# Moving the softmax sums' high parts to ScalarE and one key's row to GpSimd, with the sums' products two steps later

## The chip, the cores and the metric

One core of one Trainium2 chip. The metric is the device time of one execution in microseconds (us). The kernel before took 1920.23 us, the median of 3 runs (1919.83 to 1922.81).

## What is computed

A decoder layer: cross-attention of 16 x 56 tokens of width 256 over 1500 context tokens (16 heads of 128), then a mixture of 32 experts of which each token uses 4. The change lies in the attention alone. Cut to what matters:

```python
q = rms_norm(x @ q_w + q_b, nq_s)                    # 16 batches, 56 queries, 16 heads
k_img = rms_norm(img_ctx @ ki_w + ki_b, nki_s)       # image: context tokens 0..256 (257)
k_txt = rms_norm(txt_ctx @ k_w + k_b, nkt_s)         # text: context tokens 257..1499 (1243)
scores = q . k / sqrt(128)
attn = softmax(scores, axis=keys)                    # over image keys and text keys apart
out = sdpa(q, k_txt, v_txt) + sdpa(q, k_img, v_img)
```

Each softmax needs, per query and head, the sum of its exponentials over all keys. These sums are what the change deals with.

## The kernel before, in words

All products have 32-bit results at high precision: an operand is split into a high part, rounded to the format that TensorE multiplies fast (fp32r), and a low part, the rest; three products (high x high, low x high, high x low) stand for one.

The attention (`attend`) runs over 16 batches, `B`. A batch's context is cut into 13 tiles of up to 128 tokens: tiles 0, 1 and 2 are image, with 128, 128 and 1 token (tile 2, `LONE`, is the single key), tiles 3 to 12 are text. The 16 x 56 = 896 columns of queries and heads are taken in two halves of 448. A pair of a tile and a half is a **unit**; a batch has 26 (`UNITS`), numbered tile x 2 + half, so units 4 and 5 are the single key's. Every engine runs the same 26 **steps** per batch, with an order written out by hand in its own `body`:

- TensorE, step u: the scores of unit u (6 matmuls of 448 columns; for the single key 2), at even steps a "gram" product for the next tile (5 matmuls, lines 1150 and 1152), from which the keys' mean square comes, and the average of unit u-2 (lines 1143 to 1145 too). An ordinary unit has 12 matmuls in all, 6 for its scores and 6 for its average. The single key has no average on TensorE. The last two averages of a batch are carried into steps 0 and 1 of the next.
- ScalarE, step u: two exponentials of unit u-1, one to p_high (line 1322), one back to PSUM (1324), or one to lone_probs for the single key; c_high of a tile two ahead at even steps (`prepare`, 1303); high parts of the queries (`split_u`), copies of the averages (`copy_o`), and the copy of a sum's row out of PSUM (`copy_sum`, 1342).
- VectorE, step u: for unit u-1 (`take`) p_low (1405), the addition of the unit's exponentials to a running sum p_sum, 128 partitions x 448 (`add`, 1458 or 1461), and the copy of a bias to PSUM for a unit three ahead (`seed`, 1416). TensorE's scores of a unit wait for its seed, its average for p_low. At even steps also the mean square of a tile (`norm`, 1430, shown as junk<-psum,c_twice). It stands behind `take`, except at steps one before a sum's product (2, 4, 8, 10) and at step 6, where it stands ahead of it (`norms_first`). For the single key `take` adds lone_probs x its context row to o_raw (1447), and `add` works on one partition (1461, 1x448).
- GpSimd: at even steps key_rms (1611) of the tile whose mean square has just come; at odd steps c_low (1617) and c_twice (1630) of a tile two ahead. c_twice is the input of the next mean square. In between, at fixed steps, the query work of 128x896: `split_u` (u_low, 1661) at steps 2, 4, 12, 14, `scale_u` (1636) at 8, 10, 24 and 0, `scale_o` (1679) for the text of the batch before at 16 and 18 and for the image at 20 and 22, and `split_lone` (1667) at 17 and 19.
- SP issues the DMAs: tile loads, query loads, and the way of the sums: `store_sums`, `load_sums`, `store_reciprocals`, `load_reciprocals`, `store_o`, each at a fixed tile of its loop (`set_end`).

**The sums.** When the last unit of a half has been added, VectorE casts p_sum to its high part (`split_sum`, 1469) and subtracts to the low part (through `sub`, 1405). TensorE multiplies both with ones (`sums`, lines 1214 and 1215), into the same PSUM bank, `GRAM`, as the gram product, so it waits until the mean square of that bank has been read (`norm_summed`). ScalarE copies one row of the result, and the next gram waits for that copy (`sums_left`, `sum_copied`). The row goes to memory and back, VectorE takes reciprocals, and GpSimd multiplies the averages with them (`scale_o`). The text's sums of a batch are finished in the next batch. The steps are constants in lines 881 to 884:

```python
TEXT_SUM_SPLIT, TEXT_SUMS, TEXT_RECIP = (1, 2), (3, 5), 10
IMAGE_SUM_SPLIT, IMAGE_SUMS, IMAGE_RECIP = (7, 8), (9, 11), 16
```

The order in which the engines work in their steps is that of the calls in `body`; an engine waits in its order, and all behind a waiting instruction on it waits too.

## Time and profile before

| | before |
|---|---|
| median of 3 runs | 1920.23 us |
| the profiled execution | 1918.63 us |
| its span in the trace | 1916.8 us |
| TensorE busy (matmuls) | 1751.0 us, 91% |
| VectorE busy | 1397.1 us, 73% |
| ScalarE busy | 983.2 us, 51% |
| GpSimd busy | 1149.5 us, 60% |
| granted TensorE clock, mean | 0.973 of full |

In the tables PE is TensorE, PEld its weight loads, DVE VectorE, ACT ScalarE, POOL GpSimd, SPq the issue of DMAs from SyncE. The attention's batches run from about 250 to 1445 us; before them stand the projections, behind them the output product and the experts. Matmuls are pipelined, so a matmul's time in the trace is longer than the distance to the next; idle time counts on TensorE. The batch that the rows show begins at about 699 us and the next at about 774 us.

### The profile page before, as it was taken

Reading aid. Unit: us, or ns where it says so; the run is one execution under the profiler, and the core shown is the slowest. Engines: PE = TensorE matmul, PEld = TensorE weight load, DVE = VectorE, ACT = ScalarE, POOL = GpSimd, SP = SyncE. Lnnn points to the kernel's source line nnn. Section 1 sums busy time; section 2 is a strip of 40 time slices with the busy share of each in tenths; the row PEclk is TensorE's granted clock in tenths of the full one; section 3 lists DMA queues with packets and bytes.
Section 4 is the critical chain, followed back from the end, with each engine's and each line's share of the span. In section 5 each row is a group of like instructions: output and inputs, shape, how many; then the busy total and the mean of one; then the engine's idle time right before and its main releaser. Section 6 shows DMA issues by size and latency. Waiting matters only on the chain. (4 is left out here: it accounts for less than half of the span.)

```text
span 1916.8 us, 30691 instructions
## 1 busy us (share of the span) xinstructions
PE 1751.0 (91%) x8731; PEld 1534.5 (80%) x8731; DVE 1397.1 (73%) x2577; ACT 983.2 (51%) x1657; POOL 1149.5 (60%) x989
## 2 busy tenths in 40 slices
PE   7899979999999999999999999999992998699998
PEld 6566669889888888888898898888892886688887
DVE  4344477887978878878878879788782564577776
ACT  3444445555655655555555556556552553244443
POOL 1000278888788788788788887887862331133332
PEclk9999999999999999999999999999996999799999
DMA  3365564465564665554564665556436782133332
GB/s 110 121 208 197 194 183 111 107 116 123 123 120 114 130 121 117 122 135 114 116 132 108 116 126 125 116 116 131 98 90 195 252 274 92 66 107 115 116 109 78
DMA packets 417364, 251.19 MB, mean 131 GB/s; under 512 B 350272, under 2 KB 368832, under 8 KB 415520
## 3 DMA queue, kind: packets, MB, share of 16 engines
q1 hardware_dynamic: 417312, 250.55, 51.2%
q8 instruction: 26, 0.43, 0.1%
q14 instruction: 26, 0.21, 0.0%
HBM read 187.71 MB, written 60.10 MB: 129 GB/s over the span
## 5 line engine op out<-in xcount | busy, mean ns | idle before, releaser
L1322 ACT ACTIVATE p_high<-psum,key_rms 128x448 fp32r<-128x448 f32 x384 | 244.7, 637 | 397.1 <-PE psum L1145 397.0
L1143 PE MATMUL psum<-p_high,c_high 128*128 128x448 f32 (+1 forms) x768 | 287.8, 375 | 48.0 <-DVE p_low L1405 48.0
L1405 DVE TENSOR_TENSOR p_low<-psum,p_high 128x448 fp32r<-128x448 f32 x384 | 236.4, 616 | 100.2 <-ACT psum L1324 99.1
L1143 PE MATMUL psum<-u_high,c_high 128*128 128x448 f32 x768 | 285.5, 372 | 21.0 <-DVE psum L1416 15.1
L1144 PE MATMUL psum<-u_low,c_high 128*128 128x448 f32 x768 | 282.5, 368 | 0.0
L1145 PE MATMUL psum<-u_high,c_low 128*128 128x448 f32 x768 | 281.5, 366 | 0.0
L1145 PE MATMUL psum<-p_high,c_low 128*128 128x448 f32 (+1 forms) x768 | 281.5, 366 | 0.0
L1144 PE MATMUL psum<-p_low,c_high 128*128 128x448 f32 (+1 forms) x768 | 281.0, 366 | 0.0
L1416 DVE COPY psum<-beta_wide 128x448 f32<-128x448 f32 x416 | 259.4, 627 | 20.2 <-DMA beta_wide<-absorbed_biases 4.4
L1617 POOL TENSOR_TENSOR c_low<-stage,c_high 128x512 fp32r<-128x512 f32 x208 | 273.6, 1316 | 0.0
L1324 ACT ACTIVATE psum<-psum,key_rms 128x448 f32<-128x448 f32 x384 | 232.3, 605 | 0.0
L1611 POOL TENSOR_TENSOR key_rms<-key_ms,minus_half 128x1 f32<-128x1 f32 x209 | 118.9, 569 | 185.6 <-DVE key_ms L1430 183.3
L1143 PEld LDWEIGHTS psum<-p_high,c_high 128*128 128x128 f32 (+1 forms) x768 | 144.0, 188 | 72.8 <-DVE p_low L1405 62.1
L1461 DVE TENSOR_TENSOR p_sum<-psum,p_sum 128x448 f32<-128x448 f32 (+1 forms) x320 | 196.4, 614 | 0.0
L1143 PEld LDWEIGHTS psum<-u_high,c_high 128*128 128x128 f32 x768 | 144.8, 189 | 46.0 <-DVE psum L1416 20.6
L1630 POOL TENSOR_TENSOR c_twice<-stage,c_low 128x256 f32<-128x256 f32 x208 | 169.0, 812 | 16.3 <-POOL c_low L1617 2.4
L2024 POOL TENSOR_TENSOR scaled_gate<-gated,p_wide 128x448 f32<-128x448 f32 x64 | 83.5, 1306 | 155.8 <-ACT gated L2125 151.9
L1145 PEld LDWEIGHTS psum<-u_high,c_low 128*128 128x128 f32 x768 | 144.9, 189 | 12.5
L1145 PEld LDWEIGHTS psum<-p_high,c_low 128*128 128x128 f32 (+1 forms) x768 | 144.1, 188 | 12.1
L1430 DVE CUSTOM_DVE_ANT_0 junk<-psum,c_twice 128x257 bf16<-128x257 f32 x208 | 88.6, 426 | 89.3 <-POOL c_twice L1630 87.7
L1144 PEld LDWEIGHTS psum<-u_low,c_high 128*128 128x128 f32 x768 | 144.9, 189 | 10.9
L1144 PEld LDWEIGHTS psum<-p_low,c_high 128*128 128x128 f32 (+1 forms) x768 | 144.3, 188 | 8.6
(241 smaller groups left out, 4018.3 us busy)
## 6 DMA issues: line engine op xcount, KB each, us to landing
stage<-in_ctx SPq DMA_DIRECT2D x210, 256.0 KB, 2.8
averages<-o_raw SPq DMA_DIRECT2D x64, 448.0 KB, 5.2
o_stage<-averages SPq DMA_DIRECT2D x32, 896.0 KB, 5.4
u_raw<-absorbed_queries SPq DMA_DIRECT2D x60, 448.0 KB, 5.5
absorbed_queries<-u_stage SPq DMA_DIRECT2D x14, 1792.0 KB, 6.8
beta_wide<-absorbed_biases SPq DMA_DIRECT2D x32, 448.0 KB, 5.3
recip_wide<-reciprocals SPq DMA_DIRECT2D x32, 448.0 KB, 4.1
p_wide<-probs_by_expert SPq DMA_DIRECT2D x32, 448.0 KB, 3.6
```

What stands on the lines that cost most here:

```text
L1143: nc.tensor.matmul(out, high, rhigh, start=start, stop=False, **kw)
L1144: nc.tensor.matmul(out, high, rlow, start=False, stop=False, **kw)
L1145: return nc.tensor.matmul(out, low, rhigh, start=False, stop=stop, **kw)
L1322: nc.scalar.activation(p_high[:, probs_slot(u), :], src, ACT.Exp, scale=key_rms[:, t:t + 1])
L1324: nc.scalar.activation(out, src, ACT.Exp, scale=key_rms[:, t:t + 1]).then_inc(exp_done, 1)
L1405: return nc.vector.tensor_tensor(out, a, b, ALU.subtract)
L1416: nc.vector.tensor_copy(psum[:, bank_of(u), 0:HALF], beta_wide[:, s, cols_of(half)])\
L1430: nc.vector.tensor_tensor_reduce(out=junk[:, :], in0=psum[:, GRAM, 0:DIM + 1], in1=c_twice[:, slot(t, TWICE_RING), :], scale=1.0 / INNER, ...
L1461: added = nc.vector.tensor_tensor(total, part, total, ALU.add)
L1611: nc.gpsimd.tensor_tensor(key_rms[:, t:t + 1], key_ms[:, t:t + 1], minus_half[:, 0:1], ALU.pow)\
L1617: nc.gpsimd.tensor_tensor(c_low[:, k, :], stage[:, st, :], c_high[:, k, :].bitcast(F32), ALU.subtract)\
L1630: nc.gpsimd.tensor_tensor(c_twice[:, slot(t, TWICE_RING), 0:DIM], stage[:, st, nat], c_low[:, k, nat].bitcast(F32), ALU.add).then_inc(stag ...
```

## The change

ScalarE makes the high parts of the four sums of a batch (`high_sum`, new), at steps 1 and 2 for the text and 7 and 8 for the image; VectorE's cast is gone, its subtraction moves one step later. GpSimd adds the single key's row to the image's sums (`add_lone`, new), at steps 5 and 6; VectorE's add for it is gone, and its seeds no longer count it. The sums' products, the copies of their rows, the reciprocals and the image's scaling come two steps later. With the steps of the products, the steps at which the mean square stands ahead of `take` change too: 4, 6, 10 and 12 instead of 2, 4, 6, 8 and 10. SP's order stays.

```diff
--- before.py
+++ after.py
@@ -48,6 +48,8 @@
 PREP = 2
 UNITS = 2 * TILES
 AVERAGES = UNITS - 2
+
+ADDS = AVERAGES
 TOK = 112
 
 WB = DIM + 2
@@ -96,6 +98,11 @@
 def averaged(u):
 
     return u + 1 - min(max(u + 1 - 2 * LONE, 0), 2)
+
+
+def added(u):
+
+    return averaged(u)
 
 
 def probs_slot(u):
@@ -879,9 +886,11 @@
         O = 0
         IMAGE, TEXT = 0, 1
         TEXT_SPLIT, IMAGE_SPLIT = (1, 3), (10, 12)
+        TEXT_SUM_HIGH, IMAGE_SUM_HIGH = (1, 2), (7, 8)
+        LONE_ADDED = (5, 6)
         LONE_TERMS, LONE_HIGH, LONE_LOW = (12, 14), (14, 16), (17, 19)
-        TEXT_SUM_SPLIT, TEXT_SUMS, TEXT_RECIP = (1, 2), (3, 5), 10
-        IMAGE_SUM_SPLIT, IMAGE_SUMS, IMAGE_RECIP = (7, 8), (9, 11), 16
+        TEXT_SUM_SPLIT, TEXT_SUMS, TEXT_RECIP = (2, 3), (5, 7), 12
+        IMAGE_SUM_SPLIT, IMAGE_SUMS, IMAGE_RECIP = (8, 9), (11, 13), 18
 
         inverse_dram = nc.dram_tensor("inverse_rms", [B * TILES, 2, P], F32, kind="Internal").ap()
         negative_dram = nc.dram_tensor("negative_maxima", [B, 2 * HS // P, P], F32, kind="Internal").ap()
@@ -910,7 +919,7 @@
         u_loaded = [sem("u_image_loaded"), sem("u_text_loaded")]
         o_stored = [sem("o_image_stored"), sem("o_text_stored")]
 
-        lone_copied = sem("lone_copied")
+        lone_copied, lone_added = sem("lone_copied"), sem("lone_added")
         lone_step, lone_summed, lone_high_ready, lone_split = (
             sem("lone_step"), sem("lone_summed"), sem("lone_high_ready"), sem("lone_split"))
         u_scaled, u_high_ready, u_split = sem("u_scaled"), sem("u_high_ready"), sem("u_split")
@@ -1323,6 +1332,15 @@
                 out = lone_probs[:, half, :] if t == LONE else src
                 nc.scalar.activation(out, src, ACT.Exp, scale=key_rms[:, t:t + 1]).then_inc(exp_done, 1)
 
+            def high_sum(it, s, half):
+                n = 4 * it + 2 * s + half
+                last = 2 * (LONE if s == 0 else TILES) - 2 + half
+                act.wait_ge(sum_added, ADDS * it + added(last) + CREDIT["sum_added"])
+                if s == 0:
+                    act.wait_ge(lone_added, 2 * it + half + 1)
+                act.wait_ge(sum_wide, n - 1 + CREDIT["sum_wide"])
+                copy(p_sum_high[:, half, :], p_sum[:, 2 * s + half, :]).then_inc(sum_high_ready, 1)
+
             def split_lone(it, half):
 
                 act.wait_ge(lone_summed, 2 * it + half + 1)
@@ -1359,6 +1377,10 @@
                         carried(it, step)
                     if step >= 1:
                         exponentials(it, step - 1)
+                    if has_prev and step in TEXT_SUM_HIGH:
+                        high_sum(it - 1, TEXT, TEXT_SUM_HIGH.index(step))
+                    if step in IMAGE_SUM_HIGH:
+                        high_sum(it, IMAGE, IMAGE_SUM_HIGH.index(step))
                     if has_prev:
                         text_sums(it, step)
                     if step - 1 in IMAGE_SUMS:
@@ -1375,6 +1397,8 @@
             def tail(it):
                 for step in range(TEXT_SUMS[1] + 2):
                     carried(it, step)
+                    if step in TEXT_SUM_HIGH:
+                        high_sum(it - 1, TEXT, TEXT_SUM_HIGH.index(step))
                     text_sums(it, step)
 
             def maxima(it):
@@ -1452,21 +1476,20 @@
             def add(it, u):
                 t, half = divmod(u, 2)
                 s, n = int(t >= IMG_TILES), ROWS[t]
+                if t == LONE:
+                    return
                 part, total = probs_of(u)[0:n], p_sum[0:n, 2 * s + half, :]
                 if t in (0, IMG_TILES):
                     dve.wait_ge(sum_split, 4 * (it - 1) + 2 * s + half + 1 + CREDIT["sum_split"])
-                    added = nc.vector.tensor_copy(total, part)
+                    done = nc.vector.tensor_copy(total, part)
                 else:
-                    dve.wait_ge(sum_added, UNITS * it + u - 1 + CREDIT["sum_added"])
-                    added = nc.vector.tensor_tensor(total, part, total, ALU.add)
-                added.then_inc(sum_added, 1)
+                    dve.wait_ge(sum_added, ADDS * it + added(u) - 2 + CREDIT["sum_added"])
+                    done = nc.vector.tensor_tensor(total, part, total, ALU.add)
+                done.then_inc(sum_added, 1)
 
             def split_sum(it, s, half):
-                last = 2 * (IMG_TILES if s == 0 else TILES) - 2 + half
                 n = 4 * it + 2 * s + half
-                dve.wait_ge(sum_added, UNITS * it + last + 1 + CREDIT["sum_added"])
                 dve.wait_ge(sum_wide, n - 1 + CREDIT["sum_wide"])
-                nc.vector.tensor_copy(p_sum_high[:, half, :], p_sum[:, 2 * s + half, :]).then_inc(sum_high_ready, 1)
                 dve.wait_ge(sum_high_ready, n + 1)
                 sub(p_sum_low[:, half, :], p_sum[:, 2 * s + half, :], p_sum_high[:, half, :].bitcast(F32))\
                     .then_inc(sum_split, 1)
@@ -1501,7 +1524,7 @@
                 split_probs(it, u)
                 add(it, u)
                 if u // 2 != LONE and (has_next or u + SC_RING < UNITS):
-                    dve.wait_ge(sum_added, UNITS * it + u + 1 + CREDIT["sum_added"])
+                    dve.wait_ge(sum_added, ADDS * it + added(u) + CREDIT["sum_added"])
                     seed_after(it, u, has_next)
 
             def body(it, has_prev, has_next):
@@ -1662,6 +1685,12 @@
                                         u_high[:, 2 * s:2 * s + 2, cols].bitcast(F32), ALU.subtract)\
                     .then_inc(u_split, 1)
 
+            def add_lone(it, half):
+                gp.wait_ge(exp_done, UNITS * it + 2 * LONE + half + 1 + CREDIT["exp_done"])
+                gp.wait_ge(sum_added, ADDS * it + added(2 * LONE - 2 + half) + CREDIT["sum_added"])
+                total = p_sum[0:1, half, :]
+                nc.gpsimd.tensor_tensor(total, lone_probs[0:1, half, :], total, ALU.add).then_inc(lone_added, 1)
+
             def split_lone(it, half):
                 gp.wait_ge(lone_high_ready, 2 * it + half + 1)
                 nc.gpsimd.tensor_tensor(lone_low[:, half, :], lone_terms[:, half, :], lone_high[:, half, :].bitcast(F32),
@@ -1694,6 +1723,8 @@
                         scale_first(TEXT, 1)
                     if not has_prev and step in (1, 2):
                         split_lone(it, step - 1)
+                    if step in LONE_ADDED:
+                        add_lone(it, LONE_ADDED.index(step))
                     if has_next and step in LONE_LOW:
                         split_lone(it + 1, LONE_LOW.index(step))
                     if step in (2, 4):
@@ -1704,8 +1735,8 @@
                         split_u(it + 1, IMAGE, (step - 12) // 2)
                     if has_prev and step in (16, 18):
                         scale_o(it - 1, TEXT, (step - 16) // 2)
-                    if step in (20, 22):
-                        scale_o(it, IMAGE, (step - 20) // 2)
+                    if step in (22, 24):
+                        scale_o(it, IMAGE, (step - 22) // 2)
                     if has_next and step == 24:
                         scale_u(it + 1, TEXT, 0)
```

## Rows read from the trace of the kernel before

**Rows 1.** Busy time by stage: length, then PE, PEld, DVE, ACT, POOL (instructions), clock, DMA.

```profile
600.00:800.00 200.00, 189.63 (x982) 170.88 (x981) 163.36 (x319) 115.50 (x202) 168.23 (x147) 1.00 0.58 121
```

**Rows 2.** The list of waits from 400 to 1350 us: total, times, longest.

```profile
PEld psum L1143 <- DVE p_low L1405: 50.0, 52, 1.7
...
DVE junk L1430 <- POOL c_twice L1630: 70.0, 101, 1.1
...
PEld psum L1150 <- ACT sum_row L1295: 3.1, 13, 0.2
```

**Rows 3.** The timeline of TensorE, 700 to 730 us: start, length, line, idle before.

```profile
709.20 0.39 PE L1150 MATMUL psum<-gram_high,c_high 128*128 128x258 f32 x1
...
711.52 0.47 PE L1143 MATMUL psum<-p_high,c_high 128*128 128x448 f32 x1 [1.45 <-DVE p_low L1405]
...
719.09 0.47 PE L1143 MATMUL psum<-u_high,c_high 128*128 128x448 f32 x1 [0.89 <-DVE psum L1416]
...
721.47 0.47 PE L1143 MATMUL psum<-p_high,c_high 128*128 128x448 f32 x1 [0.28 <-DVE p_low L1405]
...
729.11 0.47 PE L1143 MATMUL psum<-p_high,c_high 128*128 128x448 f32 x1 [1.27 <-DVE p_low L1405]
```

**Rows 4.** The timeline of VectorE in the same batch, steps 2 to 6.

```profile
705.91 0.42 DVE L1430 CUSTOM_DVE_ANT_0 junk<-psum,c_twice 128x257 bf16<-128x257 f32 x1
706.25 0.62 DVE L1405 TENSOR_TENSOR p_low<-psum,p_high 128x448 fp32r<-128x448 f32 x1
...
707.97 1.34 DVE L1469 CAST p_sum_high<-p_sum 128x448 fp32r<-128x448 f32 x1
...
710.85 0.61 DVE L1405 TENSOR_TENSOR p_low<-psum,p_high 128x448 fp32r<-128x448 f32 x1
...
712.56 0.42 DVE L1430 CUSTOM_DVE_ANT_0 junk<-psum,c_twice 128x257 bf16<-128x257 f32 x1
...
718.06 0.43 DVE L1430 CUSTOM_DVE_ANT_0 junk<-psum,c_twice 128x257 bf16<-128x257 f32 x1 [0.64 <-POOL c_twice L1630]
```

**Rows 5.** Groups by line and shape, 400 to 1350 us; the last for one line.

```profile
L1405 DVE TENSOR_TENSOR p_sum_low<-p_sum,p_sum_high 128x448 fp32r<-128x448 f32 x52 | 65.0, 1250 | 1.8
...
L1469 DVE CAST p_sum_high<-p_sum 128x448 fp32r<-128x448 f32 x52 | 44.7, 859 | 0.0
...
L1667 POOL TENSOR_TENSOR x_high<-lone_terms,x_high 128x448 fp32r<-128x448 f32 x25 | 29.0, 1158 | 0.0
...
L1461 DVE TENSOR_TENSOR p_sum<-lone_probs,p_sum 1x448 f32<-1x448 f32 x26 | 22.8, 876 | 0.0
...
L1295 ACT ACTIVATE x_high<-lone_terms 128x448 fp32r<-128x448 f32 x26 | 14.7, 564 | 0.0
...
L1626 POOL TENSOR_TENSOR lone_row<-stage,zeros 128x2 f32<-128x2 f32 x13 | 3.4, 259 | 2.1 <-POOL c_low L1617 2.1
...
L1661 POOL TENSOR_TENSOR u_low<-u_raw,u_high x62: 2120/2139/2449, 261.6 to 1383.8; 128x896 fp32r<-128x896 f32 x62
```

**Rows 6.** The timeline of GpSimd in the same batch.

```profile
717.03 1.00 POOL L1630 TENSOR_TENSOR c_twice<-stage,c_low 128x256 f32<-128x256 f32 x1
...
723.98 0.55 POOL L1611 TENSOR_TENSOR key_rms<-key_ms,minus_half 128x1 f32<-128x1 f32 x1 [2.51 <-DVE key_ms L1430]
...
763.20 0.74 POOL L1630 TENSOR_TENSOR c_twice<-stage,c_low 128x256 f32<-128x256 f32 x1 [0.17 <-POOL c_low L1617]
```

**Rows 7.** The timeline of ScalarE: unit 1's exponential, and c_high at step 22.

```profile
704.69 0.64 ACT L1324 ACTIVATE psum<-psum,key_rms 128x448 f32<-128x448 f32 x1
...
760.89 0.63 ACT L1295 ACTIVATE c_high<-stage 128x512 fp32r<-128x512 f32 x1
```

**Rows 8.** The timeline of SP's DMA issues: reciprocals stored, averages stored.

```profile
747.64 0.35 SPq L992 DMA_DIRECT2D reciprocals<-recip_cols  x1
...
770.03 2.55 SPq L1004 DMA_DIRECT2D averages<-o_raw  x2
```

**Rows 9.** The page's DMA issues: count, size, us from issue to landing.

```profile
stage<-in_ctx SPq DMA_DIRECT2D x210, 256.0 KB, 2.8
```

## The prediction

> **What bounds the kernel now.** I read the stage table first: from 600 to 800 us TensorE has matmuls in flight for 189.6 of 200 us and starts 982, one per 0.204 us, at full clock; VectorE and GpSimd stand above 80% [rows 1]. So TensorE sets the pace, and only its waits can be won. The list of waits names them: products that wait for VectorE's p_low, 50.0 us over 950 us (as the weight loads see it), a few for a seed, and almost none (13 times 0.2 us) for a copied sum. VectorE itself waits 101 times for GpSimd's c_twice [rows 2]. The timeline of one batch puts every wait of TensorE into its first ten steps: 1.45 us at 711.52, 0.89 at 719.09, 0.28 at 721.47, 1.27 at 729.11, together 3.9 us [rows 3]; from there to the end of the batch it has none. Fifteen batches run with the text half of the one before them; if all these waits went, the gain would be 15 x 3.9 = 58 us. A change of 0.2%, 3.8 us, is about what a measurement can tell from none.
>
> VectorE's own rows say why. At 707.97 comes the cast of the sums' high part, 1.34 us, then the subtraction that makes the low part, and p_low of unit 2 only at 710.85, for which TensorE waits until 711.52 [rows 3, 4]. At step 6 the mean square ("junk") waits for c_twice until 718.06, and the seed behind it (line 1416) releases TensorE at 719.09 [rows 3, 4].
>
> **What is removed.** Four casts a batch at 0.86 us and two adds of the single key's row at 0.88, 5.2 us of VectorE [rows 5]. That is more than the 3.9 us of waits, but all of it isn't on their path: a second loop runs beside it. The mean square of tile t releases GpSimd's key_rms, then come its u_low, c_low and c_twice, and these release the mean square of tile t+1. From 712.56 to 718.06 one turn takes 5.50 us with c_twice at 1.00 us [rows 4, 6]. The row's add on VectorE ran over that c_twice; undisturbed one takes 0.74 [rows 6], so I take 5.50 - 0.26 = 5.25.
>
> **What is moved, step by step** (times on the clock of the batch shown).
> ScalarE gets a copy 128x448 from SBUF at steps 1 and 2; the like of it is 0.56 us [rows 5], and pushes what is behind it by about 0.5. So the exponential of unit 1, which ended at 704.69 + 0.64 = 705.33 [rows 7], ends at 705.8. The sums' steps are no longer 3 and 9, so at step 2 the mean square now stands behind unit 1 instead of ahead of it. p_low, add and seed take 707.97 - 706.25 = 1.72 us [rows 4]: the mean square of tile 2 moves from 705.91 to 707.6.
> TensorE's gram of step 4 started at 709.20 [rows 3] and takes 0.6. Without the two products of step 3 (2 x 0.204 = 0.41 us) it wants p_low of unit 2 at 709.4. VectorE has it at 709.1: mean square 0.35, an undisturbed subtraction 0.6, p_low 0.6. **The wait of 1.45 us goes.**
> But the loop started 1.7 us later. The mean square of tile 3 comes at 707.6 + 5.3 = 712.9 (was 712.56), that of tile 4 at 718.2 (was 718.06). The sum's first product, now at step 5, writes the bank that this mean square reads. TensorE is there at 709.4 + 1.2 + 0.4 = 711.0 and must wait until 713.4: **a wait of 2.4 us takes the old one's place.** The next average follows p_low of unit 3, 713.9. Scores of 6, gram and scores of 7 take it to 718.1, the second sum waits for tile 4's mean square until 718.7, and scores of unit 8 start at about 719.25, against 719.09. Up to here nothing is won.
> Then the row's adds. GpSimd has never done one; the nearest rows are the 128x448 subtraction, 1.16 us, and below it a 128x2 add, 0.26 us; above, the 128x896 operations, 2.14 us in the median [rows 5]. I take 1.16, the same columns. First add: from the end of c_twice at 718.2 to 719.35. key_rms, second add: to 721.0. ScalarE's step 7 now waits for the first, step 8 for the second, and behind step 8's high part stands the copy of the text's second sum. High part 719.4, exponential of 7 to 721.0, high part, copy: 722.0. TensorE's gram of step 8 waits for exactly that copy. It is there at 720.5: **a new wait of about 1.5 us**, where [rows 2] had 0.2.
> From 722.0 I find no wait to the end of unit 8's average: 0.6 + 4 x 1.22 + 0.6 + 1.22 = 7.3, so 729.4. p_low of 8 is ready at 725.3, since the cast and the long subtraction ahead of it are gone or later. Before, it ended at 729.11 + 0.1 + 1.22 = 730.4. That is 1.05 us, less one sum (0.41) that is still to come: **0.65 us a batch.**
>
> The Trainium skill, "SBUF — State Buffer", section "SBUF: two separate sides", says that a VectorE operation with two SBUF inputs, or in a two-port mode, and a GpSimd operation exclude each other for the whole instruction. The trace agrees: the subtraction of sums has a mean of 1250 ns and the cast 859, p_low with an input in PSUM 0.6. What I charge above goes by these rows.
> The text's second subtraction, now at about 710.2, meets u_low and may hold up c_low behind it; for that I took 5.3 instead of 5.25 for the first turn.
>
> Covered, at nothing: the image scaling on GpSimd moves from steps 20 and 22 to 22 and 24, so step 24 holds two of the 2.14 us operations, and the c_twice of the next batch's first steps comes up to 2.14 us later. The mean square of step 2 is itself 1.7 us later than before, which covers all but 0.4; VectorE's idle time at the batch's turn I take to cover the rest. If it didn't: 0.4 us a batch, 6 us. SP stores the image's reciprocals at 747.64 [rows 8]; that wait moves by two steps, 2 x 12 x 0.204 + 0.6 = 5.5 us, to about 753.1, and the tile load queued behind it has until ScalarE's c_high at 760.89 [rows 7], with a landing of 2.8 us [rows 9]. The store of the averages, 770.03 [rows 8], moves by up to 2.14 us, with the query and tile loads behind it on SP; a tile is loaded two tiles ahead, 9.8 us of matmuls, so 2.8 + 2.14 fit. If they didn't, ScalarE's c_high and TensorE's gram would be late by the rest. The text's reciprocals and the image's sums move by the same two steps as each other, so their stores and loads keep their order on SP. GpSimd's 2.3 us of adds fall where it idled 2.51 us at 723.98 [rows 6].
>
> **The sum.** 15 x 0.65 = 10 us. First batch and tail: nothing. The profiled execution took 1918.63 us (span 1916.8), 1.6 below the median 1920.23. So 1909 there, 1910.5 on the median.
>
> The Trainium skill, "GPSIMD Engine Reference", section "Performance versus the Vector engine", advises against GpSimd for elementwise work and gives 2.6 cycles an element at 1.2 GHz, which would be 0.97 us for 448 (an estimate). By it the two adds would cost 0.3 us a batch less and the sum would be 1906; the rows' 1.16 decides here.
>
> **Rivals.**
> 1. *The row's adds are cheap* (0.26 us, the 128x2 row). Then ScalarE's high parts wait hardly at all, the copied sum is there at 721.2 instead of 722.0, and the gain is 0.65 + 0.8 = 1.45 a batch: 22 us, 1898. Against it: at 128 partitions time grows with columns, 1158 ns at 448 and 259 at 2 [rows 5], and one partition hardly changes the columns. For it: only my estimates of queueing have to be a little long. Chance 0.20. All waits gone (58 us, 1862) is within it, 0.02.
> 2. *Slower: the copied sum behind the row's adds.* ScalarE, in order, holds TensorE's gram at step 8 until GpSimd has added twice. Each add lies in that chain, so each 0.1 us more on one costs 0.2 a batch; from 1.16 + 0.33 = 1.5 us per add on the kernel is slower. At 2.14 the loss is 2 x 0.98 - 0.65 = 1.3 a batch, 20 us: 1940. For it: ScalarE's order is fixed and nothing else fills TensorE there. Against it: the same columns took 1.16. Chance 0.24, with smaller losses from the later mean square, around 1927.
> 3. *Nothing to be measured:* the waits only change places. What is won at units 2 and 8 is given back at steps 5 and 8 to the last 0.25 us. Chance 0.14, at 1918 to 1922.
> That the change doesn't do what it says I see no way to: the casts and adds leave VectorE's queue in the text.
>
> **How the numbers follow.** Forecast case 0.42, 1903 to 1916; with rival 1 faster is 0.62, same 0.14, slower 0.24. The range of eight in ten takes rival 1's figure and a bit beyond, and half of rival 2's loss: 1894 to 1930.
>
> **What would show it.** VectorE's cast and its 1x448 add are gone; p_low of unit 2 releases nobody, no wait at 711.5. TensorE's first sum product (line 1214's) waits some 2.4 us for key_ms, and gram (line 1150's) some 1.5 us for sum_row, once a batch each. The mean square of tile 4 and the seed of unit 8 stand where they stood against the batch's start; unit 8's average ends 1 us earlier. A GpSimd 1x448 add of 1.16 us; at 0.3 rival 1 holds, at 1.5 or more rival 2. Wrong would be a batch period that falls by over 1.5 us, or no wait on sum_row.

## The result and the profile after

The changed kernel is slower, where the prediction had it faster.

| | before | after |
|---|---|---|
| median | 1921.30 us (4 runs) | 1943.07 us (4 runs, 1941.16 to 1943.96) |
| ratio, 95% interval | | 1.0112, 1.0094 to 1.0129 |
| profiled execution, its span | 1918.63, 1916.8 us | 1942.37, 1940.6 us |
| granted clock, whole span | 0.973 | 0.957 |

The page of the changed kernel first, its line of busy time:

```profile
PE 1771.4 (91%) x8731; PEld 1559.3 (80%) x8731; DVE 1324.6 (68%) x2481; ACT 1017.2 (52%) x1721; POOL 1184.8 (61%) x1021
```

VectorE has lost 72 us of work, as the change intends, ScalarE has 34 more and GpSimd 35. TensorE issues the same work as before and is busy 20 us longer. The list of waits of the changed kernel from 400 to 1350 us (total, times, longest), for comparison with [rows 2]:

```profile
DVE junk L1454 <- POOL c_twice L1653: 156.8, 101, 2.7
POOL key_rms L1634 <- DVE key_ms L1454: 124.3, 135, 3.3
...
PE psum L1223 <- DVE key_ms L1454: 36.6, 14, 2.8
...
PE psum L1159 <- ACT sum_row L1304: 8.3, 13, 1.2
...
PE psum L1152 <- DVE p_low L1429: 7.4, 12, 0.7
```

Before, the matmuls' own line for p_low was:

```profile
PE psum L1143 <- DVE p_low L1405: 38.7, 39, 1.5
```

So the old wait has shrunk from 38.7 to 7.4 us, 0.6 a time. In its place stand the sum's product (line 1223), which waits for the mean square 2.6 us a time, and the gram, which waits for sum_row. VectorE's waits for c_twice have more than doubled, from 70.0 to 156.8 us. TensorE's timeline has all three waits of one batch:

```profile
721.68 0.74 PE L1223 MATMUL psum<-p_sum_high,ones_r 128*128 128x448 f32 x1 [2.81 <-DVE key_ms L1454]
...
731.55 0.39 PE L1159 MATMUL psum<-gram_high,c_high 128*128 128x258 f32 x1 [0.57 <-ACT sum_row L1304]
...
750.66 0.47 PE L1152 MATMUL psum<-p_high,c_high 128*128 128x448 f32 x1 [0.64 <-DVE p_low L1429]
```

Together 4.0 us, against 3.9 before: by its waits alone this batch would hardly be longer. The stages around the first wait show what is missing (length, then busy time of PE, PEld, DVE, ACT, POOL, the granted clock, DMA):

```profile
715.00:718.00 3.00, 3.00 (x19) 2.81 (x18) 2.97 (x8) 2.43 (x5) 2.45 (x3) 1.00 1.17 236
718.00:721.00 3.00, 0.86 (x5) 0.46 (x3) 1.23 (x1) 1.68 (x3) 2.92 (x3) 0.98 0.85 172
721.00:724.00 3.00, 2.32 (x6) 2.13 (x7) 2.68 (x7) 0.53 (x1) 2.45 (x3) 0.50 0.34 103
724.00:727.00 3.00, 3.00 (x9) 2.69 (x9) 1.14 (x2) 0.63 (x1) 2.92 (x4) 0.50 0.00 0
727.00:730.00 3.00, 3.00 (x17) 2.81 (x17) 1.72 (x5) 2.18 (x5) 1.66 (x3) 0.88 0.31 87
730.00:735.00 5.00, 4.42 (x24) 3.79 (x23) 4.93 (x11) 3.01 (x7) 3.15 (x4) 1.00 0.21 54
```

Right behind the wait the granted clock is 0.50, 1.2 instead of 2.4 GHz. PE is shown busy for all of 724 to 727, but starts 9 matmuls there; from 715 to 718, at full clock, it starts 19. A busy share does not tell these two apart, the count and the clock do.

The batch shown is one of the three that lose most. Behind the 15 waits of 2.80 to 3.08 us for the mean square, one in each batch but the first, the clock is at half for 6.8 us in three batches, for 3.4 us in eleven, and in one not at all:

```profile
646.73 0.47 PE L1223 MATMUL psum<-p_sum_high,ones_r 128*128 128x448 f32 x1 [2.80 <-DVE key_ms L1454]
...
655.29 0.39 PE L1159 MATMUL psum<-gram_high,c_high 128*128 128x258 f32 x1 [1.24 <-ACT sum_row L1304]
```

```profile
646.00:649.00 3.00, 2.27 (x10) 1.78 (x11) 2.63 (x7) 0.74 (x2) 2.45 (x3) 1.00 0.33 87
649.00:652.00 3.00, 2.86 (x17) 2.35 (x15) 1.67 (x6) 1.56 (x3) 2.92 (x4) 1.00 0.00 0
```

This batch takes 75.1 us; those with 3.4 us at half clock take 75.4 to 76.6, the three with 6.8 us 76.8 to 77.0, and those of the kernel before, after its first, 74.4 to 74.9. At full clock its waits are 2.80, 1.24 and 0.36 us, together 4.4: the half clock hides a part of the later ones. What decides between the three cases these runs don't show.

VectorE in the same batch, steps 0 to 14:

```profile
709.75 0.43 DVE L1454 CUSTOM_DVE_ANT_0 junk<-psum,c_twice 128x257 bf16<-128x257 f32 x1 [2.66 <-POOL c_twice L1653]
...
715.26 0.43 DVE L1454 CUSTOM_DVE_ANT_0 junk<-psum,c_twice 128x257 bf16<-128x257 f32 x1
...
717.87 1.36 DVE L1429 TENSOR_TENSOR p_sum_low<-p_sum,p_sum_high 128x448 fp32r<-128x448 f32 x1
721.19 0.43 DVE L1454 CUSTOM_DVE_ANT_0 junk<-psum,c_twice 128x257 bf16<-128x257 f32 x1 [1.96 <-POOL c_twice L1653]
...
745.02 0.43 DVE L1454 CUSTOM_DVE_ANT_0 junk<-psum,c_twice 128x257 bf16<-128x257 f32 x1 [1.39 <-POOL c_twice L1653]
...
747.20 1.23 DVE L1502 TENSOR_SCALAR lone_terms<-u_raw,lone_keys 128x448 f32<-128x448 f32 x1
748.57 1.49 DVE L1505 SCALAR_TENSOR_TENSOR lone_terms<-u_raw,lone_keys,lone_terms 128x448 f32<-128x448 f32 x1
...
753.42 0.42 DVE L1454 CUSTOM_DVE_ANT_0 junk<-psum,c_twice 128x257 bf16<-128x257 f32 x1
```

and GpSimd:

```profile
718.70 1.65 POOL L1640 TENSOR_TENSOR c_low<-stage,c_high 128x512 fp32r<-128x512 f32 x1
...
726.33 1.13 POOL L1692 TENSOR_TENSOR p_sum<-lone_probs,p_sum 1x448 f32<-1x448 f32 x1
...
746.05 2.13 POOL L1684 TENSOR_TENSOR u_low<-u_raw,u_high 128x896 fp32r<-128x896 f32 x1
...
753.92 0.69 POOL L1634 TENSOR_TENSOR key_rms<-key_ms,minus_half 128x1 f32<-128x1 f32 x1 [3.27 <-DVE key_ms L1454]
...
780.18 2.13 POOL L1708 TENSOR_TENSOR o_raw<-o_raw,recip_wide 128x896 f32<-128x896 f32 x1
782.27 2.13 POOL L1659 TENSOR_TENSOR u_raw<-u_raw,rms_batch 128x896 f32<-128x896 f32 x1
```

Three things are to be seen. The mean square of step 0 (709.75) already waits 2.66 us for c_twice. At step 12 it stands ahead of the unit's work (745.02), lets u_low start at 746.05, and the single key's two terms, which VectorE does behind it, take 1.23 and 1.49 us; the mean square of step 14 comes at 753.42, and GpSimd has waited 3.27 us for it. At step 24 GpSimd has two of the 2.13 us operations in a row.

**The loop's turns.** The prediction followed one loop: mean square on VectorE, then key_rms, the query work, c_low and c_twice on GpSimd, then the next mean square. A batch has 13 turns of it. Read from the starts of line 1454 (1430 before) in one batch of each kernel, the distance from one mean square to the next, in us; e1 to e16 are the experiments below. The row of the changed kernel is of the long batch shown above: over its batches the turn at 4 is 5.3 to 7.2 us and the sum 75.9 in the mean, 1.5 us or 22 us in 15 batches more than before, while the turns from 6 on agree within 0.05 us but in the first and last batches.

| kernel | 0 | 2 | 4 | 6 | 8 | 10 | 12 | 14 to 18 | 20 | 22 | 24 | sum |
|---|---|---|---|---|---|---|---|---|---|---|---|---|
| before | 5.93 | 6.65 | 5.50 | 5.41 | 6.68 | 5.57 | 5.73 | 16.66 | 5.86 | 5.26 | 5.27 | 74.5 |
| after | 5.51 | 5.93 | 7.09 | 5.50 | 5.97 | 5.27 | **8.40** | 16.66 | 3.80 | 5.27 | **7.35** | 76.8 |
| e4 shift only | 5.48 | 5.86 | 6.05 | 6.15 | 5.90 | 5.26 | 8.38 | 16.66 | 3.79 | 5.25 | 7.35 | 76.1 |
| e12 | 5.50 | 5.99 | 5.24 | 5.50 | 5.95 | 5.27 | 8.39 | 16.65 | 3.80 | 5.26 | 7.34 | 74.9 |
| e15 | 5.50 | 6.03 | 5.25 | 5.50 | 5.95 | 5.51 | 5.78 | 16.66 | 4.77 | 5.50 | 7.34 | 73.8 |
| e2 | 5.48 | 5.98 | 5.23 | 4.82 | 6.02 | 5.49 | 6.97 | 16.67 | 4.22 | 5.49 | 7.32 | 73.7 |
| e7 | 5.48 | 5.99 | 5.25 | 4.77 | 6.03 | 5.49 | 5.78 | 16.67 | 4.85 | 5.49 | 7.33 | 73.1 |
| e13 | 5.92 | 5.64 | 5.26 | 5.05 | 5.65 | 5.57 | 5.70 | 16.63 | 4.53 | 5.49 | 7.32 | 72.8 |
| e3 no shift | 5.68 | 5.63 | 5.25 | 5.05 | 5.64 | 5.58 | 5.71 | 16.65 | 5.88 | 5.26 | 5.24 | 71.6 |

### The profile page after: what moved, and what is told of

It is laid out like the page before. It is cut to its first block and busy times, and to the rows that moved or that the text cites. A ratio compares the mean times of both kernels' runs of the same rounds, so it can differ in the third digit from the quotient of the medians.

```text
span 1940.6 us, 31249 instructions
## 1 busy us (share of the span) xinstructions
PE 1771.4 (91%) x8731; PEld 1559.3 (80%) x8731; DVE 1324.6 (68%) x2481; ACT 1017.2 (52%) x1721; POOL 1184.8 (61%) x1021
## 5 line engine op out<-in xcount | busy, mean ns | idle before, releaser
L1153 PE MATMUL psum<-p_low,c_high 128*128 128x448 f32 (+1 forms) x768 | 286.6, 373 | 0.0
L1154 PE MATMUL psum<-p_high,c_low 128*128 128x448 f32 (+1 forms) x768 | 286.3, 373 | 0.0
L1640 POOL TENSOR_TENSOR c_low<-stage,c_high 128x512 fp32r<-128x512 f32 x208 | 282.5, 1358 | 0.0
L1634 POOL TENSOR_TENSOR key_rms<-key_ms,minus_half 128x1 f32<-128x1 f32 x209 | 127.0, 607 | 174.5 <-DVE key_ms L1454 171.9
L1653 POOL TENSOR_TENSOR c_twice<-stage,c_low 128x256 f32<-128x256 f32 x208 | 157.7, 758 | 16.3 <-POOL c_low L1640 2.4
```

What stands on the lines that cost most here:

```text
L1153: nc.tensor.matmul(out, high, rlow, start=False, stop=False, **kw)
L1154: return nc.tensor.matmul(out, low, rhigh, start=False, stop=stop, **kw)
L1634: nc.gpsimd.tensor_tensor(key_rms[:, t:t + 1], key_ms[:, t:t + 1], minus_half[:, 0:1], ALU.pow)\
L1640: nc.gpsimd.tensor_tensor(c_low[:, k, :], stage[:, st, :], c_high[:, k, :].bitcast(F32), ALU.subtract)\
L1653: nc.gpsimd.tensor_tensor(c_twice[:, slot(t, TWICE_RING), 0:DIM], stage[:, st, nat], c_low[:, k, nat].bitcast(F32), ALU.add).then_inc(stag ...
```

## The experiments

In the expectations Theory A and Theory B (and, from e13 on, C and D) are spelled out for each run. "Shift" means the later steps of the sums' subtraction, products, copies, reciprocals and image scaling with the mean square's places that follow from them; "the two moves of work" are the high parts on ScalarE and the row's add on GpSimd. Ratios are to the kernel before, run on the same chip in the same job, with 95% intervals. Every kernel computes all of the layer; e1 also multiplies a tile of zeros. The diffs are cut to the lines that matter.

**e4, the shift alone**, in the kernel before:

```diff
-        TEXT_SUM_SPLIT, TEXT_SUMS, TEXT_RECIP = (1, 2), (3, 5), 10
-        IMAGE_SUM_SPLIT, IMAGE_SUMS, IMAGE_RECIP = (7, 8), (9, 11), 16
+        TEXT_SUM_SPLIT, TEXT_SUMS, TEXT_RECIP = (2, 3), (5, 7), 12
+        IMAGE_SUM_SPLIT, IMAGE_SUMS, IMAGE_RECIP = (8, 9), (11, 13), 18
...
-                    if step in (20, 22):
-                        scale_o(it, IMAGE, (step - 20) // 2)
+                    if step in (22, 24):
+                        scale_o(it, IMAGE, (step - 22) // 2)
```

> The kernel before with nothing changed but the steps: subtraction and cast one step later, products, reciprocals and image scaling two steps later, the mean square's places with them. Theory A: slower than the kernel before, 1925 to 1950 us, with a wait for key_ms at the first text sum behind a wait for p_low. Theory B (shift harmless): 1915 to 1922.

Measured: 1941.01 us, ratio 1.0107 (1.0090 to 1.0124), inside Theory A's range and 2 us under the kernel with all of the change. But the loss is made up otherwise. Its long wait for the mean square is 2.5 us, and the clock falls behind it in 7 of 15 batches, each time for 3.4 us, not in 14 (timeline of TensorE, and a stage behind the wait in such a batch):

```profile
722.67 0.47 PE L1214 MATMUL psum<-p_sum_high,ones_r 128*128 128x448 f32 x1 [2.47 <-DVE key_ms L1430]
```

```profile
724.00:727.00 3.00, 3.00 (x10) 2.68 (x9) 3.00 (x5) 0.65 (x2) 2.92 (x3) 0.52 0.18 68
```

Its batches with the fall take 76.1 us, those without 75.6. Part of what the clock gives back here, the turn at 6 takes, 6.15 us with the casts on VectorE and 5.50 without.

**e3, the two moves of work without the shift**: the changed kernel with the four lines of e4's diff put back.

> High parts on ScalarE and the key's row on GpSimd as in the change, but the subtractions, sums' products, reciprocals and image scaling at their old steps. Theory A (the two moves of work are good, the shift of the products is what costs, since it moves the mean square): no fall of the clock at step 5, no wait on sum_row at step 8, time 1880 to 1900 us. Theory B (work on ScalarE and GpSimd costs by itself): slower than before, 1925 to 1945.

Measured: 1877.14 us (1873.46 to 1882.23), ratio 0.9770 (0.9753 to 0.9786), 43 us faster than before, 66 faster than the changed kernel, and 3 us below the range of Theory A. The clock does not fall. TensorE keeps two waits a batch, 0.82 us for sum_row at 695.68 (the gram of step 4, where Theory A spoke of step 8 alone), and 0.51 for a seed at 703.38. So the moves gain more than the prediction ever gave them, and the shift costs 66 us.

**e5 and e6, the moves one at a time**, both without the shift. e5 is the kernel before with `high_sum` and without VectorE's cast, the row's add left on VectorE; e6 is e3 with the cast back in `split_sum` and `high_sum` gone.

> Old steps, high parts on ScalarE, the single key's row still on VectorE. Theory A (GpSimd's loop, started by the mean square, and p_low behind the casts bound steps 2 to 10): most of the 43 us that both moves gave without the shift come from here, since the casts stand ahead of p_low; 1880 to 1895 us. Theory B (the row's add is what matters): 1905 to 1918.

> Old steps, the single key's row on GpSimd, casts still on VectorE. Theory A: the waits at steps 4 and 10 behind the casts stay, the one at step 8 shrinks by some 0.3 us a batch; 1908 to 1920 us. Theory B (GpSimd's adds cost by themselves, as rival 2 had it): over 1922.

Measured: e5 1880.69 us, ratio 0.9800 (0.9783 to 0.9816); e6 1911.44 us (8 runs, 1909.17 to 1916.71), ratio 0.9955 (0.9944 to 0.9967). Both lie in Theory A's ranges. The casts are worth 41 us and the row's add 9 to 10; together, 43, they give hardly more than the casts alone. In e6 the turns at steps 2 and 8, those of the casts, are still 6.64 and 6.66, as before; in e5 they are 5.63 and 5.65. That is the 2 us a batch.

**e1, the same waits at full clock.** To the changed kernel 12 products of a zero tile are added, into a bank of running averages (they add zeros), ahead of the text's first sum product, where TensorE would wait:

```diff
                 pe.wait_ge(sum_copied, n + CREDIT["sum_copied"])
+                if fill:
+                    pe.wait_ge(start_ready, 3)
+                for _ in range(fill):
+                    nc.tensor.matmul(psum[:, O + 2, 0:HALF], idle_zero[:, :], p_sum_high[:, half, :],
+                                     start=False, stop=False, skip_group_check=True)
```

> The changed kernel with 12 matmuls of a zero tile (adding nothing to the averages) ahead of the text's first sum product, where TensorE now waits 2.8 us for key_ms once a batch. No other engine's work changes. Theory A (the loss is TensorE's clock, which falls to 0.50 right behind that wait and stays there for some 5.5 us a batch): the wait falls to about 0.4 us, the granted clock stays at 1.00, the batch period falls from 75.1 to 76.9 us back to about 74.4, the time to 1915 to 1925 us. Theory B (the loss lies in the waits themselves or in ScalarE's and GpSimd's added work): the clock may change but the time stays within 5 us of the changed kernel, 1938 to 1948.

Measured: 1931.25 us (1930.09 to 1931.49), ratio 1.0056 (1.0039 to 1.0073), so 12 us less than the changed kernel, by adding work. It lies between the two ranges: Theory A had the mechanism and gave it 6 us too much. The clock falls in no batch; in the stage where it had been 0.50 it is 1.00:

```profile
721.00:724.00 3.00, 2.92 (x17) 2.38 (x16) 1.71 (x6) 1.59 (x3) 2.92 (x4) 1.00 0.00 0
```

and TensorE's timeline now has the wait for sum_row at its full length, with only 0.41 us left ahead of the sum's product:

```profile
718.75 0.47 PE L1231 MATMUL psum<-p_sum_high,ones_r 128*128 128x448 f32 x1 [0.41 <-DVE key_ms L1462]
...
727.28 0.39 PE L1162 MATMUL psum<-gram_high,c_high 128*128 128x258 f32 x1 [1.25 <-ACT sum_row L1312]
```

The changed kernel is at half speed for 11 x 3.4 + 3 x 6.8 = 58 us in all, so TensorE does 29 us of work less in them; but the half clock had hidden a part of the second wait (0.57 against 1.25), and at full clock only 12 us come back, 12 / 15 = 0.8 us a batch. After the first two, the batches of e1 take 75.0 us in the mean; the one batch of the changed kernel that kept its clock takes 75.1. So it is the clock that the products buy, and not something else that they do.

**e2, the mean square in its old places**, the sums' steps shifted:

```diff
-                    norms_first = step % 2 == 0 and (step + 1 in TEXT_SUMS + IMAGE_SUMS or step == 2 * LONE + 2)
+                    norms_first = step in (2, 4, 6, 8, 10)
```

> The changed kernel with the mean square ahead of VectorE's take at steps 2, 4, 6, 8 and 10, as in the kernel before, and not at 12. Theory A (the mean square of step 2 stands 1.7 us late, starts GpSimd's loop late, and so makes the wait at the first sum product long enough to lose the clock): wait at the first text sum under 1 us, no fall of the clock, GpSimd's loop 1.7 to 2 us earlier at step 4 and 6, time 1885 to 1905 us. Theory B (order of the mean square is of no account, the loss comes from the sums' new places or the added work): 1935 to 1945.

Measured: 1909.22 us, ratio 0.9946 (0.9929 to 0.9963), 34 us less than the changed kernel, in the direction of Theory A, but 4 us above its range. The clock is 1.00. Four waits are left a batch: 0.58 and 0.63 for p_low, 0.35 for the mean square, 1.26 for sum_row.

**e12 and e15, which of the three places it is.** The changed kernel has the mean square ahead of the unit at steps 4, 6, 10 and 12, the old order is 2, 4, 6, 8 and 10. e12 puts back step 2 alone, e15 steps 2 and 12; what then parts e15 from e2 is step 8 (the comments name the run).

```diff
+                    norms_first = step in (2, 4, 6, 10, 12)    # e12
+                    norms_first = step in (2, 4, 6, 10)        # e15
```

> The changed kernel with one edit: the mean square of step 2 ahead of VectorE's take again; those of steps 8 and 12 stay where the change put them. Theory A (the mean square of step 2 is what makes the long wait and loses the clock; that of step 12 costs a wait of some 0.7 us for p_low by itself, 10 us in all): the clock stays at 1.00, the wait at step 12 stays, time 1912 to 1926 us, between the changed kernel and the second run. Theory B (all of it is step 2): as the second run, 1904 to 1911. Theory C (all of it is step 12 or 8): 1935 to 1945.

> Kernel: the changed one with the mean square ahead of the unit's work at steps 2, 4, 6 and 10: against the run with steps 2, 4, 6, 10 and 12 (1929 us) only step 12 is put back. Theory C (at step 12 the early mean square lets u_low start ahead of VectorE's single-key terms, which then take 1.22 and 1.50 us and hold the next mean square; the turn 12 to 14 is 8.4 us): the turn shrinks to 7.0 or less and the time to 1905 to 1912. Rival: step 8's place carries it, the time stays at 1922 or more.

Measured: e12 1928.63 us, ratio 1.0037 (1.0022 to 1.0051), 3 us above what Theory A expected; e15 1910.36 us, ratio 0.9937 (0.9920 to 0.9954). e15 lies in Theory C's range. Step 2 is worth 14 us, of which e1 gives 12 to the clock; step 12 is worth 18; step 8 nothing that can be measured. In e12 the one long wait has become three, 1.13 and 0.62 us for p_low and 0.34 for the mean square, and the clock stays at 1.00. e15's timeline of VectorE at step 12, where the single key's terms had taken 1.23 and 1.49 us:

```profile
729.50 0.42 DVE L1454 CUSTOM_DVE_ANT_0 junk<-psum,c_twice 128x257 bf16<-128x257 f32 x1
729.84 0.20 DVE L1512 RECIPROCAL recip_cols<-sum_cols 112x8 f32<-112x8 f32 x1
729.95 0.40 DVE L1502 TENSOR_SCALAR lone_terms<-u_raw,lone_keys 128x448 f32<-128x448 f32 x1
730.50 0.69 DVE L1505 SCALAR_TENSOR_TENSOR lone_terms<-u_raw,lone_keys,lone_terms 128x448 f32<-128x448 f32 x1
```

In the table the turn at 12 falls from 8.39 to 5.78, 2.6 us, but the sum by only 1.1: the turn at 20 grows from 3.80 to 4.77 and the one at 22 by 0.24. Between steps 14 and 22 the loop catches up what it lost, until it stands again where TensorE holds it; only what is lost beyond that is lost for the batch. TensorE shows most of this remainder as a wait for p_low at step 12 (0.36 us in e12, none over 0.3 in e15) and in a first wait for p_low of 1.13 us instead of 0.62 in the next batch.

**e16, the order of a 0.2 us instruction.** In e2 the second term still took 2.49 us, since the text's reciprocals (moved from step 10 to 12) stand ahead of the terms and u_low had started 0.11 ahead of it:

```profile
730.39 2.12 POOL L1684 TENSOR_TENSOR u_low<-u_raw,u_high 128x896 fp32r<-128x896 f32 x1
...
730.50 2.49 DVE L1505 SCALAR_TENSOR_TENSOR lone_terms<-u_raw,lone_keys,lone_terms 128x448 f32<-128x448 f32 x1
```

e16 is e2 with the reciprocals behind the terms.

```diff
                 if step in TEXT_SUM_SPLIT:
                     split_sum(it - 1, TEXT, TEXT_SUM_SPLIT.index(step))
-                if step == TEXT_RECIP:
-                    reciprocals(it - 1, TEXT)
...
                         terms_of_lone(it + 1, LONE_TERMS.index(step))
+                    if has_prev and step == TEXT_RECIP:
+                        reciprocals(it - 1, TEXT)
...
```

> Kernel: the changed one with the mean square in its old places (1909 us, 73.7 us a batch), with the text's reciprocals at step 12 behind the single-key terms instead of ahead of them. Theory C (0.2 us of reciprocals is enough to let u_low start ahead of the second term, which then takes 2.49 us instead of 0.69): that term is back at 0.7, the turn 12 to 14 falls from 6.97 to 5.8 and the time to about 1895 to 1901. Rival (GpSimd's loop has slack there and the term covers nothing): within 3 us of 1909.

Measured: 1910.53 us, ratio 0.9941 (0.9925 to 0.9958), so nothing, as the rival had it, though the term is back at 0.68 us and the turn at 12 at 5.85. The turn at 20 took it up (5.31 instead of 4.22). So here the loop can lose a good microsecond at step 12 for nothing; the changed kernel's 8.40 goes beyond that, and in e14, below, even this microsecond counts.

**e7, the text's copy ahead of the high part** on ScalarE, in e2:

```diff
+                    if has_prev:
+                        text_sums(it, step)
                     if has_prev and step in TEXT_SUM_HIGH:
                         high_sum(it - 1, TEXT, TEXT_SUM_HIGH.index(step))
                     if step in IMAGE_SUM_HIGH:
                         high_sum(it, IMAGE, IMAGE_SUM_HIGH.index(step))
-                    if has_prev:
-                        text_sums(it, step)
```

> The second run (shifted, but the mean square in its old places) with ScalarE's copy of the sum ahead of the next high part instead of behind it. Theory A (the gram of step 8 waits 1.25 us because the copy stands behind a high part that waits for GpSimd's add): that wait goes to under 0.3 us, the batch gets up to 1.2 us shorter, time 1890 to 1903 us. Theory B (something else would stop TensorE there anyway, GpSimd's loop for instance): 1905 to 1911, the wait moves to a seed or to key_ms.

Measured: 1901.37 us, ratio 0.9904 (0.9888 to 0.9921). The time lies in Theory A's range, though the wait for sum_row only falls from 1.26 to 0.65 us where Theory A had under 0.3. The time falls by 8 us with it: 0.6 us in each of 14 batches. This part of the prediction's chain (gram behind copy behind high part behind add) holds.

**e13, the image's scaling alone two steps later**, in e3:

```diff
-                    if step in (20, 22):
-                        scale_o(it, IMAGE, (step - 20) // 2)
+                    if step in (22, 24):
+                        scale_o(it, IMAGE, (step - 22) // 2)
```

> Kernel: the one with the two moves of work and no shift (1877 us, 71.6 us a batch), with the image's scaling on GpSimd alone two steps later (22 and 24 instead of 20 and 22). Theory C (the turns of the loop mean square - GpSimd - c_twice decide the batch): the turn from step 20 to 22 shrinks from 5.88 only to about 4.9, because VectorE's queue holds the mean square there, while the turn from 24 to 0 grows from 5.24 to 7.3; net 1.0 to 1.3 us a batch, 15 to 19 us: 1892 to 1896. Theory D (what the shift still costs, 24 us, lies in the places of the sums' products; GpSimd's total is unchanged and the late scaling is covered, as the prediction had it): within 4 us of 1877.

Measured: 1893.05 us (1892.52 to 1897.78), ratio 0.9856 (0.9839 to 0.9872), 16 us more than e3, as Theory C had it. GpSimd does the same work in the batch, but in another order: the turn at 24 grows by 2.08, the turn at 20 shrinks by 1.35 only, because there the mean square waits for TensorE and VectorE and no longer for c_twice. The timeline of VectorE shows both, no wait for c_twice at step 22, and at step 0 behind the two long operations:

```profile
750.40 0.43 DVE L1454 CUSTOM_DVE_ANT_0 junk<-psum,c_twice 128x257 bf16<-128x257 f32 x1
755.89 0.43 DVE L1454 CUSTOM_DVE_ANT_0 junk<-psum,c_twice 128x257 bf16<-128x257 f32 x1
763.21 0.43 DVE L1454 CUSTOM_DVE_ANT_0 junk<-psum,c_twice 128x257 bf16<-128x257 f32 x1 [1.92 <-POOL c_twice L1653]
```

**e14, the image's part back at its old steps**, the text's still late: e7 with the image's lines of e4's diff put back.

> Kernel: the shifted one with the mean square in its old places and the text's copy ahead of the high part (1901 us), with the image's part (subtractions, products, reciprocals, scaling) back at its old steps; the text's part stays two steps late. Theory C: the turns 20 to 22 and 24 to 0 are as without a shift, 5.9 and 5.2, and the time is 1878 to 1886. Theory D: the text's products at 5 and 7 carry half or more of the remaining 24 us: 1889 or more.

Measured: 1886.29 us (1882.28 to 1893.66), ratio 0.9805 (0.9789 to 0.9822). 15 of the 24 us between e7 and e3 go with the image's part, as many as e13 gives to its scaling; the median lies 0.3 us above Theory C's range and below Theory D's. The other 9 us belong to the text's part, and the profile shows two places. In three batches the sum is 71.8 us, 0.25 more than in e3: the turns at 0 and 2 are 5.49 and 6.01 (e3: 5.68, 5.63), and a wait of 0.67 for sum_row and 0.35 for the mean square are left. In eleven others the sum is 73.0, and all of the difference is the turn at 12, 6.98 instead of 5.8: there the text's reciprocals again stand ahead of the single key's terms, and the second term takes 2.54 us:

```profile
577.73 2.12 POOL L1684 TENSOR_TENSOR u_low<-u_raw,u_high 128x896 fp32r<-128x896 f32 x1
...
577.78 2.54 DVE L1505 SCALAR_TENSOR_TENSOR lone_terms<-u_raw,lone_keys,lone_terms 128x448 f32<-128x448 f32 x1
```

In e2 the turn at 20 took this up (4.22 against 5.31 in e16); here that turn is 5.88 in both kinds of batch and takes up nothing. 11 x 1.1 us are 12 us of the profiled execution, which is the slowest of the four (1893.66); how many batches the others lose so wasn't seen. A kernel with the reciprocals moved alone was not tried.

**e8 to e11, what bounds the fastest ones.** e8 is e3 with the text's copy of the sum's row ahead of the step's exponential, e9 the same in e5. e10 and e11 are e8 and e9 with the low part of the single key's term on VectorE instead of GpSimd (`low_of_lone`, for `split_lone`, 2.3 us a batch less on GpSimd).

```diff
+                    if has_prev:
+                        text_sums(it, step)
                     if step >= 1:
                         exponentials(it, step - 1)
...
-                    if has_prev:
-                        text_sums(it, step)
```

> The third run (old steps) with ScalarE's copy of a text sum ahead of the step's exponential. Theory A: TensorE's gram at step 4 no longer waits 0.82 us for sum_row, time 1864 to 1874 us. Theory B (GpSimd, busy for 90% of the batch, bounds it now): 1874 to 1880, with the wait moved to a seed.

> The fifth run (old steps, high parts on ScalarE, the key's row on VectorE) with the copy of a text sum ahead of the step's exponential. Theory A (GpSimd's loop is what bounds the last two versions; here it is 2.3 us a batch lighter than with the adds on it): the wait for sum_row at step 4 goes and the batch falls from 71.8 us by up to 0.8, 1867 to 1878 us. Theory B (GpSimd doesn't bind; the copy's place did nothing in the eighth run because other waits take over): 1878 to 1883.

> The eighth run with the low part of the single key's term (2 x 1.16 us a batch on GpSimd, steps 17 and 19) on VectorE. Theory A (GpSimd, 90% busy plus 0.55 us at each mean square, bounds the batch of 71.6 us): shorter by up to 2.3 us a batch, 1845 to 1868 us. Theory B (TensorE's own waits in steps 2 to 10 bound it, GpSimd has slack later): same within 4 us, 1873 to 1881.

> The ninth run's kernel with the same low part on VectorE: GpSimd 4.6 us a batch lighter than in the eighth run. Theory A: only TensorE's waits are left, 1843 to 1868 us. Theory B: as the ninth run within 4 us.

Measured:

| | median, us | ratio | turns at 16, 18, 20 | sum |
|---|---|---|---|---|
| e8 | 1876.94 | 0.9776 (0.9759 to 0.9792) | 5.26, 5.76, 5.88 | 71.6 |
| e9 | 1881.76 | 0.9803 (0.9785 to 0.9821) | 5.26, 5.80, 5.88 | 71.8 |
| e10 | 1874.11 (1869.25 to 1877.36) | 0.9759 (0.9742 to 0.9775) | 5.64, 5.65, 5.35 | 71.3 |
| e11 | 1877.18 | 0.9765 (0.9748 to 0.9781) | 5.66, 5.65, 5.36 | 71.6 |

e8 takes the wait for sum_row away and gains nothing: seeds and p_low are waited for instead (0.67 and 0.24 us). Each of the four had a Theory A that freeing the copy or GpSimd would shorten the batch further; all four measured times lie above its range (e11's in neither range, 4.6 us below e9). In e3 the loop has hardly any slack left, by its list of waits from 400 to 1350 us: GpSimd waits for the mean square 0.6 us a time, and never over 0.9:

```profile
POOL key_rms L1634 <- DVE key_ms L1454: 77.1, 133, 0.9
```

But GpSimd's work isn't what bounds these kernels: in e10 it has 2.3 us a batch less to do, and the turns give back only 0.3. What does was not found.

e3, e8 and e10 can't be told apart by their times; each beats both kernels by 2.2% or more.

## Why the prediction was wrong, step by step

The step that failed is "0.65 us a batch". The batch became 1.5 us longer in the mean (75.9 against 74.45), and the sum had three parts of that wrong: a long wait charged by its length alone, "From 722.0 I find no wait", and "Covered, at nothing".

**Mechanisms that held.** "The wait of 1.45 us goes": it is gone. "A wait of 2.4 us takes the old one's place": 2.81 at the sum's product. The mean square of tile 2 was to move by 1.7 us; counted from the batch's first copy of averages on ScalarE (700.68 before, 708.40 after) it moved from +5.23 to +6.86, by 1.63, though by then it had a second reason to be late (step 3). The row's add was taken at 1.16 us and takes 1.14 on the mean of 26, so rival 2's price was not paid, and rival 1's not either. That rival 2's 1940 us lies near the measured 1943 is chance. (With an add at 0.97 us, the prediction's other figure, its own chain gives 0.4 us a batch less, not 0.3.) A wait of about 1.5 us for sum_row came out at 0.57 behind the half clock and at 1.24 to 1.25 without it (e1, and the changed kernel's batch at full clock). Even the total of the waits, 4.0 us a batch, is near what the sum had.

**Step 1 that failed: the wait was charged by its length.** "A wait of 2.4 us takes the old one's place" was set off against 1.45 us as like against like. The trace of before could not show the difference: TensorE's matmuls wait 1.45 us at most there [rows 3], and the clock is 1.00 from 600 to 800 us [rows 1]. Behind 2.8 us the clock fell to half in 14 of 15 batches, for 3.4 or 6.8 us, and behind e4's 2.5 in 7 of 15. By e1 that is 12 us.

**Step 2: the mean square at step 12 had no term.** The diff moves it at three steps; "What is moved, step by step" worked out step 2 and passed over 8 and 12. At 8 nothing came of it. At 12 it lets GpSimd's u_low start ahead of VectorE's single-key terms (before, it started 0.24 us behind the start of the second); these go from 0.45 and 0.69 us to 1.23 and 1.49, the turn from 5.73 to 8.40, and p_low, behind them in VectorE's order, makes the wait of 0.64 us at 750.66. "From 722.0 I find no wait" is where the forecast stopped looking. By e12 against e15 that is 18 us.

The Trainium skill, "SBUF — State Buffer", section "SBUF: two separate sides", says that of a VectorE and a GpSimd operation that exclude each other the one that starts first keeps the other out for its whole length. The trace agrees: started at 730.50, just behind a u_low of 730.39, the second term took 2.49 us in e2; in e15 it started at 730.50 ahead of a u_low of 730.73 and took 0.69, and u_low 2.44 instead of 2.13.

**Step 3: "Covered, at nothing".** The two long operations of step 24 were seen, put at 2.14 us, and taken as covered but for 0.4, because the mean square of step 2 would be late anyway. What was missed is step 0: its mean square comes 2.05 us later against the batch's first copy (from 0.70 us ahead of it to 1.35 behind), waits 2.66 us for c_twice, and VectorE's queue, p_low of the last units in it, waits with it. At step 2 the late loop and the changed order then meet: c_twice ended at 715.22, the mean square started at 715.26. So each alone puts it there, and taking one away moves it little: in e12 the mean square in its old place waits for c_twice until 708.64, 6.64 us behind that batch's first copy, 0.22 earlier. That e12 still gains 14 us comes from what stands behind the mean square: p_low is later, TensorE stops for it earlier, and the long wait is cut in three. Measured without the other effects the scaling's two steps cost 16 us (e13).

**Step 4, small: "5.3 instead of 5.25".** The text's second subtraction took 1.36 us beside u_low, and c_low behind it 1.65 instead of 1.31. The turn at step 2 is 5.93, 0.6 more than taken, and this is enough to bring the first wait from 2.4 to 2.8.

**The ledger.** From 1943 back to 1877 us, one part at a time and in this order: step 2's place with the clock 14 us, step 12's place 18, step 8's 1, the copy's order 8, the image's part 15, the text's part 9, with rounding the whole 66. The forecast was 33 us too low. Steps 1 and 2 make 30 of them. Step 3's 16 were measured where the mean square kept its old places; what they are on top of the changed kernel's other delays, and how much the wait for sum_row that came out 0.9 us shorter than forecast gives back, was not measured separately, so the whole does not close to the microsecond.

**Why the moves of work showed nothing.** With the shift they are worth nothing (e4 1941.0, after 1943.1), without it 43 us. The table shows where the gain goes: with the shift the long turns at 12 and 24 are the same with and without the moves (8.38 and 8.40, 7.35 and 7.35). The casts now lengthen the turn at 6 (6.15 against 5.50), and this the moves do win back; but with them the first wait is 2.8 us instead of 2.5 and the clock falls in 14 batches instead of 7. In e1, at full clock, the kernel with the moves is at 1931, 10 us under e4, of which e4's own clock falls are 7 x 0.5 us, an estimate from its batches. The forecast had the sign of this step the wrong way round too: it credited the moves with 1.05 us at unit 8 and never set them against an unshifted kernel, in which they bring 2.9 us a batch.

## What to carry to other kernels

When a change moves steps, work out every place in every engine's order that moves with them, also those that follow from a derived condition, and walk the slowest cross-engine loop once around the whole period rather than to the first point where it looks level. A list of distances from one turn of that loop to the next, made for before and after, finds the long turns at once, and shows where lost time is caught up (at step 20 here) and where not. Moving work off a queue and moving the steps of its consumers are two changes: here the first was worth 43 us and the second cost 66.

## What the hardware showed that was not expected

- A single wait of TensorE of 2.8 us, once in a batch of 75 us, was followed by a granted clock of 0.50 in 14 of 15 batches, for 3.4 us in eleven and 6.8 us in three; one of 2.5 us in 7 of 15 (e4). Waits of 1.5 us and less, up to 3.9 us of them in ten steps, were not, in any kernel here between 300 and 1400 us. The same wait cost nothing in one batch and some 1.8 us in three others, so one batch of a trace does not give its price. Twelve products with a zero tile in place of the wait kept the clock at 1.00 and made the kernel 12 us faster.
- A 1x448 add on GpSimd took 1.14 us in the mean, as long as a 128x448 subtraction, 1.16.
- VectorE's single-key terms (0.45 and 0.69 us alone) took 1.23 and 1.49 with u_low started ahead of both. The second took 2.48 to 2.55 in the batches in which u_low had started 0.05 to 0.11 us ahead of it (e2, e14), and 0.69 where u_low started 0.2 us or more behind it. In e16 undoing this was worth nothing, since the loop had slack behind it; in e14, without the slack, each case made the batch 1.1 us longer. A stretched instruction is a reason to look, not yet a cost.
